# One group of edges moved, routing in four chunks, and a last dense tile by column halves

## The chip, the cores and the metric

The program runs on one core of one Trainium2 chip, as one launch. The metric is device time in microseconds (us) of a whole execution. Three runs of the kernel before took 1525.8, 1527.35 and 1531.21 us; the median is 1527.35 us.

## The reference, cut to what matters

The input is 1250 nodes of 1024 features and 40,000 edges sorted by destination. Three blocks share one normalized input: a graph convolution in two layers, a linear attention with 16 heads (8 pairs here), and behind both a mixture of 8 experts in which each node goes to two.

```
xn = layernorm(x)
# graph: agg[dst] += xw[src] * dinv[src] * dinv[dst], two layers, batch norm between them
g  = relu(gcn(relu(batchnorm(gcn(xn + pe, W1))), W2))
# attention, per head:  q' = relu(q @ proj), k' = relu(k @ proj)
m  = (q' @ (k'^T v)) / (q' @ sum(k') + 1e-8), then @ Wo + bo
x  = x + g + m
# experts: logits = layernorm(x) @ Wr^T; the two highest, softmax of the two
x  = x + sum over the two of  weight * (silu(gate) * value) @ W2[e]^T
```

## The kernel before, in words

**Numbers.** Products are in float32 as three products of a high and a low part (`COMBOS`): the low part is what is left of the value when the high one is taken off. So a tile that leaves PSUM is read twice, by ScalarE for the high part and after it by VectorE for the low one. Nodes come in 10 tiles of 125 (`NT`, `T`), features in 8 blocks of 128 (`KD`).

**Order.** `steps()` writes out one list, `ORDER`, of keys such as `("Q", 3)`. Each engine walks this list and takes the keys that it has a part in, strictly in this order. `FULL`, `ACTED` and `DVED` number them, and engines wait on semaphores for these numbers. Two large PSUM tensors (`slot`) alternate; `places_of()` gives each key its slot. A key in `INNER` takes the slot that isn't the current one and does not turn the alternation over. `free_slot` makes TensorE wait until the former content of the slot has been read.

**Edges.** The adjacency matrix is built from 80 groups of 500 edges. `EO` (VectorE) makes eight one-hot tiles for a group, `group_product` (TensorE, L1605) multiplies them in four matmuls into one of two small PSUM tensors, `E` (ScalarE) copies the result to a stage, and GpSimd adds it in DRAM (L811), one at a time. `groups_within()` shares the groups over the large products. Within a slab product (`slab_product`, L1728) the groups stand behind the blocks that `PARTS` names; those past the fourth are put elsewhere by `EP`.

**Attention pair.** For pair p: keys' features `KK` and their sums `KV`, query features `QP`, transposes `S`, then the key projection `K` of pair p+1 (5 groups: four inside, the fifth by `EP` behind it), `AT(p,0)`, query features `QP(p,1,0)` and `QP(p,1,1)`, one in each slot, and the query projection `Q` of pair p+1 (2 groups inside, behind blocks 3 and 6), with `AT(p,1)` inside. `Q(p+1)` uses the slot of `QP(p,1,0)`.

**Dense tiles.** Behind the second graph layer, `N(i)` is the dense product of node tile i: 8 blocks x 3 combinations x 2 column halves = 48 matmuls of 512 columns (L1876). VectorE then adds input and attention (`xm`, for tile i made ahead), bias (`acc<-slot,b2b`), takes relu and sum (L1449), statistics (L1452, L1454), `LN2` (square root on ScalarE, one Newton step), and `FL` writes the normalized tile `flat`. `FT(i)` transposes it on TensorE (L1671, 8 transposes), and both engines evict it into `big`. In the list `FT(i-1)` stands behind `N(i)`, and takes the other slot; so `N(i+1)` has the slot of `N(i)`.

**Routing.** `CHUNKS` splits the ten tiles into (0-3), (4-6), (7-9). Per chunk: `R` router product (L1889, 16 matmuls of up to 500 columns; for the last chunk 16 over two tiles and 16 over the last tile), ScalarE copies it to `lgt`; `RT` transposes it (L1615) and ScalarE copies it to `lg`; `RK` ranks (VectorE, seven operations up to `sel`); `PX` counts earlier nodes of each expert by small matmuls over all earlier tiles (L1630 to L1644); `RW` makes the weights, with an exponential on ScalarE; `SL` makes the list positions `spots`. GpSimd then issues one scatter per tile and choice into `list_d` (L836). When all 20 have landed, SP reads the eight lists (L770), GpSimd gathers the nodes of an expert (L856), and TensorE begins with their transposes (L1932). While this goes on, SP loads the first expert weights.

## Time and profile before

| | us |
|---|---|
| median of three runs | 1527.35 |
| profiled execution, device time | 1526.58 |
| its span, first to last instruction | 1524.9 |
| TensorE busy in the span | 1423.5 |
| VectorE busy | 846.3 |
| ScalarE busy | 531.2 |
| GpSimd busy | 183.0 |

The rows are of the profiled execution. Its device time is 1.7 us above its span and 0.8 us below the median of the runs. PE is TensorE, PEld its weight loads, DVE is VectorE, ACT ScalarE, POOL GpSimd, and SP the engine that issues most transfers. Times in a trace are counted from the first instruction.

### The profile page before, as it was taken

The numbers are of one execution on the slowest core, as the hardware profiler recorded it, in microseconds if no ns is written. First come the engines' busy times: TensorE is split into PE (matmuls) and PEld (weight loads), VectorE is DVE, ScalarE is ACT, GpSimd is POOL, SyncE is SP. The second block draws the span as 40 slices with busy tenths as digits, with TensorE's granted clock in tenths as the row PEclk, the third lists the DMA queues.
The fourth block names the chain that finished last, engine by engine and source line by source line (L and its number), as shares of the span: only waits on it lengthen the run. The fifth ranks groups of instructions, "written<-read, shape, count | busy, mean of one in ns | idle before, by whom it ended". The sixth has DMA issues, their size and how long they took to land.

```text
span 1524.9 us, 20038 instructions
## 1 busy us (share of the span) xinstructions
PE 1423.5 (93%) x7735; PEld 1307.4 (86%) x7735; DVE 846.3 (55%) x1535; ACT 531.2 (35%) x617; POOL 183.0 (12%) x182
## 2 busy tenths in 40 slices
PE   6999899999999999999999999999999839999996
PEld 5888889889998898899999999999777639888885
DVE  7464677777777777723666323354667534443330
ACT  4333344354344444423112133322111134544441
POOL 0112210110100101000000000000002252222311
PEclk9999999999999999999999999999999859999998
DMA  9765333242331434768343032221654667887863
GB/s 311 233 160 120 64 62 73 37 81 60 59 78 27 94 78 130 277 150 221 85 131 84 15 110 94 81 80 45 189 158 134 161 175 201 206 218 194 189 153 78
DMA packets 97186, 194.33 MB, mean 127 GB/s; under 512 B 31715, under 2 KB 62426, under 8 KB 95373
## 3 DMA queue, kind: packets, MB, share of 16 engines
q1 hardware_dynamic: 76324, 145.83, 32.6%
q0 software_dynamic: 20768, 47.22, 17.1%
q8 instruction: 62, 1.02, 0.3%
q14 instruction: 32, 0.26, 0.1%
HBM read 129.78 MB, written 73.13 MB: 133 GB/s over the span
## 4 chain that ended last, share of the span: by engine, by line
PE 69%; DMA 13%; DVE 8%; ACT 4%; issue 2%; SPq 1%; POOL 1%; POOLq 0%; ACTq 0%; DVEq 0%
PE slot L1728 24%; PE slot L1800 12%; DMA adj_d<-stage 7%; PE slot L1949 7%; PE slot L1876 6%; PE slot L1917 6%; PE kvb L1949 3%; PE kvb L1840 3%; PE slot L1932 2%; DMA adj_d<-eye_dram 2%; PE slot L1684 2%; PE slot L1825 1%; DMA mix_d<-mixn 1%; DVE qp_l L1407 1%; DVE kT L1139 1%
## 5 line engine op out<-in xcount | busy, mean ns | idle before, releaser
L1728 PE MATMUL slot<-big_hi,slab_h 128*128 128x418 f32 x768 | 195.9, 363 | 18.2 <-DVE qp_l L1407 12.0
L1728 PE MATMUL slot<-big_lo,slab_h 128*128 128x418 f32 x768 | 188.9, 354 | 0.0
L1728 PE MATMUL slot<-big_hi,slab_l 128*128 128x418 f32 x768 | 187.8, 352 | 0.0
L1728 PEld LDWEIGHTS slot<-big_hi,slab_h 128*128 128x128 f32 x768 | 138.8, 189 | 26.5 <-DVE qp_l L1407 16.1
L1728 PEld LDWEIGHTS slot<-big_hi,slab_l 128*128 128x128 f32 x768 | 144.8, 189 | 2.3
L1728 PEld LDWEIGHTS slot<-big_lo,slab_h 128*128 128x128 f32 x768 | 144.7, 189 | 2.0
L811 POOL DMA_DIRECT2D adj_d<-stage x80 | 67.1, 839 | 504.4 <-ACT stage L891 367.4
L1800 PE MATMUL slot<-adj,xs_h 125*128 125x418 f32 x480 | 118.2, 354 | 0.8 <-DVE ztmp L1139 0.5
L1800 PE MATMUL slot<-adj,xs_l 125*128 125x418 f32 x480 | 117.4, 353 | 0.0
L1143 DVE TENSOR_SCALAR oh_src<-lane,src_lo 125x125 bf16<-125x125 f16 x320 | 82.9, 259 | 29.2 <-PE kvb L1605 19.3
L1800 PEld LDWEIGHTS slot<-adj,xs_h 125*128 125x128 f32 x480 | 90.4, 189 | 2.2 <-DVE ztmp L1139 0.7
L1800 PEld LDWEIGHTS slot<-adj,xs_l 125*128 125x128 f32 x480 | 90.5, 189 | 1.2
L836 POOL DMA_INDIRECT list_d<-rec,spots x20 | 25.7, 1284 | 542.2 <-issue 513.1
L1143 DVE TENSOR_SCALAR oh_key<-key_iota,key_rel 125x240 bf16<-125x240 int16 x320 | 89.7, 281 | 0.0
L1139 DVE TENSOR_TENSOR ws_l<-ws_raw,ws_h 128x1024 fp32r<-128x1024 f32 x32 | 38.9, 1218 | 85.6 <-ACT ws_h L891 85.6
L1421 DVE RECIPROCAL nrm<-nrm 128x1254 f32<-128x1254 f32 x8 | 63.9, 7993 | 22.6 <-ACT nrm L891 22.6
L1139 DVE TENSOR_TENSOR slab_l<-slab_raw,slab_h 128x1024 fp32r<-128x1024 f32 x34 | 41.4, 1218 | 56.4 <-ACT slab_h L891 56.4
L871 POOL DMA_INDIRECT out_dram<-y,lists x32 | 49.1, 1533 | 180.8 <-ACT y L891 175.0
L1390 DVE SCALAR_TENSOR_TENSOR kk_l<-slot,kk_h 125x512 fp32r<-125x512 f32 x80 | 51.5, 686 | 29.0 <-ACT kk_h L1024 28.5
L1949 PE MATMUL slot<-xe_h,ws_h 128*128 128x420 f32 x176 | 64.4, 366 | 2.0 <-DVE xe_l L1139 2.0
L1949 PE MATMUL slot<-xe_l,ws_h 128*128 128x420 f32 x176 | 63.0, 358 | 0.0
L1949 PE MATMUL slot<-xe_h,ws_l 128*128 128x420 f32 x176 | 62.9, 357 | 0.0
(292 smaller groups left out, 2916.1 us busy)
## 6 DMA issues: line engine op xcount, KB each, us to landing
slab_raw<-slabs_dram SPq DMA_DIRECT2D x40, 512.0 KB, 3.8
ws_raw<-w_dram SPq DMA_DIRECT2D x36, 512.0 KB
adj_d<-stage POOLq DMA_DIRECT2D x81, 117.2 KB, 3.1
w_raw<-w_dram SPq DMA_DIRECT2D x9, 1024.0 KB
adj_d<-eye_dram POOLq DMA_DIRECT2D x1, 6250.0 KB, 24.2
raw<-adj_d SPq DMA_DIRECT2D x3, 1828.8 KB
dx<-x_dram SPq DMA_DIRECT2D x10, 448.0 KB
xn_d<-dx SPq DMA_DIRECT2D x10, 448.0 KB
```

Of the source, the lines that this page charges most:

```text
L811: pool.dma_start(adj_d[:, bass.ds(first, SPAN), :].rearrange("p d j -> p (d j)"), stage[g % 3][:, :], accum_op=ALU.add).then_inc(e_added, 16)
L871: pool.indirect_dma_start(out, bass.IndirectOffsetOnAxis(ap=lists[:, e, i, 0:1].bitcast(U32), axis=0), y[i][:, :], None, compute_op=ALU.ad ...
L1139: return dve.tensor_tensor(o, a, b, op)
L1143: dve.tensor_scalar(o, a, s1, None, op0)
L1390: dve.scalar_tensor_tensor(out=kk_p[k[2] % 3][1][:, :], in0=kk_bank(k), scalar=0.0, in1=kk_p[k[2] % 3][0][:, :].bitcast(F32), op0=ALU.max, ...
L1421: link(dve.reciprocal(nrm[:, :], nrm[:, :]))
L1728: mm = ten.matmul(ps[:, 512 * q:512 * q + CW], w[a][:, kt, :], big[b][:, kt, CW * q:CW * q + CW], start=(kt == 0 and c == 0), stop=(kt == ...
L1800: mm = ten.matmul(ps[:, 512 * q:512 * q + CW], xs_p[t % 2][a][:, j, :], adj[:, j, CW * q:CW * q + CW], start=(j == 0 and a == 0), stop=(j ...
L1840: mm = ten.matmul(kvb[:, FEAT * h:FEAT * h + FEAT], v_p[a][:, i, 64 * h:64 * h + 128], kk_p[i % 3][b][:, FEAT * h:FEAT * h + FEAT], start= ...
L1876: mm = ten.matmul(ps[:T, 512 * q:512 * q + 512], big[b][:, kt, T * i:T * i + T], rows_p[kt][a][:, 512 * q:512 * q + 512], start=(kt == 0 a ...
L1917: mm = ten.matmul(to[:RT_, 512 * q:512 * q + 512], a_p[a][:, f, RT_ * i:RT_ * i + RT_], w2_p[e % 2][b][:, f, 512 * q:512 * q + 512], start ...
L1949: mm = ten.matmul(ps, w[a][:, kt, :], xe[b][:, kt, :], start=(kt == 0 and c == 0), stop=(kt == KD - 1 and c == 2))
```

## The change

- In each of the pairs 1 to 7, the key projection takes 6 groups and the query projection 1. The sixth group is multiplied behind `QP(p,1,1)`, in front of the query projection; the one left in the query projection stands behind block 5. `EO` for the sixth comes in front of the eviction of `K`.
- `FT(i-1)` stands in front of `N(i)` in the list, and is issued by TensorE inside `N(i)`: behind block 5 (behind block 6 in tile 1, behind block 2 of the second half in tile 9). It is in `INNER`, so `N` alternates between the slots.
- Four chunks: (0-3), (4-6), (7-8), (9). `RT(1)` and `PX(1)` are inside `N(8)`. `R(2)` follows `N(9)`; `RT`, `RK`, `RW` of chunk 2 stand in front of `FT(9)`. The last chunk's router product has the tokens as the stationary operand, so its result needs no transpose. `RW` is split: `RX` is its part behind the exponential. `PX` reads a running count (`counts`) in one matmul in place of one for each earlier tile.
- The last dense product goes by column halves: 24 matmuls for the first half, then 24 for the second. `NA` on VectorE treats the first half meanwhile.

```diff
-CHUNKS = ((0, 4), (4, 7), (7, 10))
+CHUNKS = ((0, 4), (4, 7), (7, 9), (9, 10))
...
-        share[("K", p)], share[("Q", p)] = 5, 2
+        share[("K", p)], share[("Q", p)] = 6, 1
...
-PARTS = {0: (), 2: (3, 6), 4: (3, 4, 6, 7), 5: (2, 3, 5, 6)}
+PARTS = {0: (), 1: (5,), 4: (3, 4, 6, 7), 6: (2, 3, 5, 6)}
...
-        behind = WITHIN[("K", p + 1)][4]
+        first, second = WITHIN[("K", p + 1)][4:]
         o += with_split(("K", p + 1), [("VL", p + 1)], copied=2)
-        o += [("AT", p, 0), ("EP", behind), ("E", behind), ("QP", p, 1, 0), ("QP", p, 1, 1)]
+        o += [("AT", p, 0), ("EP", first), ("E", first), ("QP", p, 1, 0), ("QP", p, 1, 1),
+              ("EP", second), ("E", second)]
         o += with_split(("Q", p + 1), [("AT", p, 1)], copied=0) + [("RC", p)]
...
+    in_front = {6: [("RT", 0), ("RK", 0)], 7: [("PX", 0), ("RW", 0), ("RX", 0), ("SL", 0)],
+                8: [("RT", 1), ("RK", 1), ("RW", 1), ("RX", 1)], NT - 1: [("NA", NT - 1)]}
     for i in range(NT):
-        if i == 6:
-            o += [("RT", 0), ("RK", 0)]
-        if i == 7:
-            o += [("PX", 0), ("RW", 0), ("SL", 0)]
-        if i == 9:
-            o += [("RT", 1), ("RK", 1)]
-        o.append(("N", i))
+        o += in_front.get(i, [])
         if i:
             o.append(("FT", i - 1))
-        o += [("LN2", i), ("FL", i)]
-        if i == 5:
-            o.append(("R", 0))
         if i == 8:
-            o.append(("R", 1))
-    o += [("PX", 1), ("RW", 1), ("SL", 1), ("FT", NT - 1), ("R", LAST), ("RT", LAST), ("RK", LAST), ("PX", LAST),
-          ("RW", LAST), ("SL", LAST)]
+            o += [("PX", 1), ("SL", 1)]
+        o += [("N", i), ("LN2", i)]
+        if i == NT - 1:
+            o.append(("R", 2))
+        o.append(("FL", i))
+        if i in (5, 7):
+            o.append(("R", (i - 5) // 2))
+    o += [("RT", 2), ("RK", 2), ("RW", 2), ("FT", NT - 1), ("PX", 2), ("RX", 2), ("SL", 2),
+          ("R", LAST), ("RK", LAST), ("RW", LAST), ("PX", LAST), ("RX", LAST), ("SL", LAST)]
...
+INNER |= {("FT", i) for i in range(NT - 1)}
+AMID = {(6, 3): ("RT", 0), (7, 3): ("PX", 0), (8, 1): ("RT", 1), (8, 6): ("PX", 1)}
 PSUM_KINDS = {"DG", "DT", "Z", "H", "HT", "XT", "V", "K", "Q", "KK", "QP", "AT",
...
                 elif kind == "R":
                     a, b = CHUNKS[k[1]]
+                    if k[1] == LAST:
+                        copy(lg2[:, 2 * EXP * a:2 * EXP * b], ps[:T, 0:2 * EXP]).then_inc(act_done, 1)
+                        continue
                     if k[1]:
...
+                elif k == ("N", NT - 1):
+                    i = k[1]
+                    half = slice(512, D)
+                    dve.wait_ge(psum_full, u)
+                    tt(acc[i % 2][:, half], ps[:T, half], b2b[:, half], ALU.add).then_inc(dve_done, 1)
+                    dve.wait_ge(dve_done, DVED[k])
+                    link(dve.scalar_tensor_tensor(out=acc[i % 2][:, half], in0=acc[i % 2][:, half], scalar=0.0,
+                                                  in1=xm[i % 2][:, half], op0=ALU.max, op1=ALU.add))
+                    link(dve.bn_stats(l2st[:, i, 6:12], acc[i % 2][:, half]))
+                    link(dve.bn_aggr(l2mv[:, 2 * i:2 * i + 2], l2st[:, i, :].rearrange("p (q c) -> p q c", c=6)))
+                    ts(nw[:T, 6 * i:6 * i + 1], l2mv[:, 2 * i + 1:2 * i + 2], LN_EPS, ALU.add).then_inc(ln2_var, 1)
...
+                elif kind == "NA":
+                    i = k[1]
+                    half = slice(0, 512)
+                    dve.wait_ge(acc_stored[i % 2], LAND * (i // 2))
+                    dve.wait_ge(xm_landed[i % 2], 2 * LAND * (i // 2 + 1))
+                    link(tt(xm[i % 2][:, :], xm[i % 2][:, :], x_t[i % 2][:, :], ALU.add))
+                    dve.wait_ge(dense_half, 1)
+                    link(tt(acc[i % 2][:, half], sums[SLOT[("N", i)]][:T, half], b2b[:, half], ALU.add))
+                    link(dve.scalar_tensor_tensor(out=acc[i % 2][:, half], in0=acc[i % 2][:, half], scalar=0.0,
+                                                  in1=xm[i % 2][:, half], op0=ALU.max, op1=ALU.add))
+                    dve.bn_stats(l2st[:, i, 0:6], acc[i % 2][:, half])
+                elif kind in ("RK", "RW", "RX", "SL"):
...
+                        if c < LAST:
+                            link(dve.tensor_reduce(count_f, sel[:, 0:EXP * b].rearrange("p (j e) -> p e j", e=EXP),
+                                                   AX.X, ALU.add))
+                            dve.tensor_copy(counts[:, EXP * c + EXP:EXP * c + 2 * EXP], count_f).then_inc(counted, 1)
+                    elif kind == "RX":
...
+            def router_product(k):
+
+                a, b = CHUNKS[k[1]]
+                free_slot(k)
+                ps = sums[SLOT[k]]
+                first = T * a - (T * (b - a)) % 2
+                ten.wait_ge(dve_done, DVED[("FT", b - 1)])
+                if k[1] == LAST:
+                    for kt in range(KD):
+                        for q in range(2):
+                            mm = ten.matmul(ps[:T, 0:2 * EXP], big[q][:, kt, T * a:T * b],
+                                            wr_p[q][:, 2 * EXP * kt:2 * EXP * kt + 2 * EXP],
+                                            start=(kt == 0 and q == 0), stop=(kt == KD - 1 and q == 1))
+                    mm.then_inc(psum_full, 1)
+                    return
+                for kt in range(KD):
+                    for q in range(2):
+                        mm = ten.matmul(ps[:, 0:T * b - first], wr_p[q][:, 2 * EXP * kt:2 * EXP * kt + 128],
+                                        big[q][:, kt, first:T * b],
+                                        start=(kt == 0 and q == 0), stop=(kt == KD - 1 and q == 1))
+                mm.then_inc(psum_full, 1)
...
-                    ten.wait_ge(dve_done, DVED[("RK", c - 1)])
-                    for j in range(a):
-                        ten.matmul(to.rearrange("p (j e) -> p j e", e=EXP), before_t[:, T:],
-                                   sel[:, EXP * j:EXP * j + EXP].unsqueeze(1).to_broadcast([T, b - a, EXP]),
-                                   start=(j == 0), stop=False, skip_group_check=True)
-                        if c == LAST:
-                            ten.matmul(kvb[:T, 384:384 + EXP], before_t[:, T:], sel[:, EXP * j:EXP * j + EXP],
-                                       start=False, stop=False, skip_group_check=True)
+                    ten.wait_ge(counted, c)
+                    count = counts[:, EXP * c:EXP * c + EXP]
+                    ten.matmul(to.rearrange("p (j e) -> p j e", e=EXP), before_t[:, T:],
+                               count.unsqueeze(1).to_broadcast([T, b - a, EXP]),
+                               start=True, stop=False, skip_group_check=True)
+                    if c == LAST:
+                        ten.matmul(kvb[:T, 384:384 + EXP], before_t[:, T:], count,
+                                   start=False, stop=False, skip_group_check=True)
...
+                    if i == NT - 1:
+                        for q in range(2):
+                            for kt in range(KD):
+                                for c, (a, b) in enumerate(COMBOS):
+                                    mm = ten.matmul(ps[:T, 512 * q:512 * q + 512], big[b][:, kt, T * i:T * i + T],
+                                                    rows_p[kt][a][:, 512 * q:512 * q + 512],
+                                                    start=(kt == 0 and c == 0), stop=(kt == KD - 1 and c == 2))
+                                if q and kt == 2:
+                                    token_transposes(("FT", i - 1))
+                            mm.then_inc((dense_half, psum_full)[q], 1)
+                        continue
...
-                        if i in AMID and kt == 3:
-                            (logit_transposes if AMID[i][0] == "RT" else prefix_products)(AMID[i])
+                        if kt == KD - 1:
+                            mm.then_inc(psum_full, 1)
+                        if (i, kt) in AMID:
+                            inner = AMID[i, kt]
+                            (logit_transposes if inner[0] == "RT" else prefix_products)(inner)
+                        if i and kt == (6 if i == 1 else 5):
+                            token_transposes(("FT", i - 1))
+                    continue
...
```

## Rows read from the trace of the kernel before

**Rows 1.** The page: busy us (share) and instructions of each engine.

```profile
PE 1423.5 (93%) x7735; PEld 1307.4 (86%) x7735; DVE 846.3 (55%) x1535; ACT 531.2 (35%) x617; POOL 183.0 (12%) x182
```

**Rows 2.** Stretches: us, busy us of each engine (instructions), granted clock, DMA share, GB/s.

```profile
1202.00:1240.00 38.00, 10.35 (x75) 9.90 (x73) 16.73 (x53) 7.98 (x11) 18.29 (x16) 0.60 0.50 131
1210.00:1212.00 2.00, 2.00 (x11) 2.00 (x10) 1.26 (x7) 1.01 (x1) 0.41 (x1) 0.50 0.92 295
1214.00:1216.00 2.00, 1.50 (x14) 1.35 (x13) 0.00 (x0) 0.47 (x1) 1.43 (x2) 1.00 0.97 330
1224.00:1226.00 2.00, 0.00 (x0) 0.00 (x0) 0.31 (x1) 1.99 (x3) 1.69 (x2) 0.50 0.29 62
```

**Rows 3.** TensorE's waits: for whom, us in total, times, longest.

```profile
PE slot L1728 <- DVE qp_l L1407: 12.0, 14, 1.4
PE slot L1876 <- DVE acc L1139: 3.9, 6, 1.3
```

**Rows 4.** Timeline, PE, a query projection: start, us, what, idle before.

```profile
342.70 0.85 PE L1728 MATMUL slot<-big_hi,slab_h 128*128 128x418 f32 x3 [1.38 <-DVE qp_l L1407]
...
352.58 0.73 PE L1728 MATMUL slot<-big_hi,slab_l 128*128 128x418 f32 x3
353.14 0.57 PE L1605 MATMUL lsb<-oh_key,oh_src 125*125 125x240 bf16 x4
...
354.14 0.74 PE L1728 MATMUL slot<-big_lo,slab_h 128*128 128x418 f32 x3
```

**Rows 5.** Page: the one-hot group; its columns end in busy us, mean ns.

```profile
L1143 DVE TENSOR_SCALAR oh_key<-key_iota,key_rel 125x240 bf16<-125x240 int16 x320 | 89.7, 281 | 0.0
```

**Rows 6.** Timeline, DVE, eviction of the key projection.

```profile
335.48 2.94 DVE L1139 TENSOR_TENSOR kT<-slot,kT 64x1254 fp32r<-64x1254 f32 x2 [3.58 <-ACT kT L891]
```

**Rows 7.** Timeline, PE, dense tiles 2 and 3.

```profile
1093.98 0.73 PE L1876 MATMUL slot<-slab_h,big_hi 128*125 128x512 f32 x2 [1.25 <-DVE acc L1139]
...
1105.29 1.02 PE L1671 MATMUL slot<-ident,flat 125*128 125x125 f32 x8
1106.83 0.73 PE L1876 MATMUL slot<-slab_h,big_hi 128*125 128x512 f32 x2 [0.53 <-DVE acc L1139]
```

**Rows 8.** Timeline, DVE, dense tile 0: bias to normalized tile.

```profile
1085.15 1.23 DVE L1139 TENSOR_TENSOR acc<-slot,b2b 125x1024 f32<-125x1024 f32 x1 [1.53 <-DMA b2b<-b_rows_dram]
...
1090.72 0.81 DVE L1142 TENSOR_SCALAR flat<-acc,l2mv,rstd 125x1024 f32<-125x1024 f32 x1
```

**Rows 9.** Timeline, DVE, dense tile 9, the same two operations.

```profile
1201.63 1.22 DVE L1139 TENSOR_TENSOR acc<-slot,b2b 125x1024 f32<-125x1024 f32 x1 [2.22 <-PE slot L1876]
...
1207.85 0.81 DVE L1142 TENSOR_SCALAR flat<-acc,l2mv,rstd 125x1024 f32<-125x1024 f32 x1
```

**Rows 10.** Timeline, all engines, transposes of tile 9 and their eviction.

```profile
1208.81 1.90 PE L1671 MATMUL slot<-ident,flat 125*128 125x125 f32 x8 [6.08 <-DVE flat L1142]
...
1210.74 1.01 ACT L891 ACTIVATE big_hi<-slot 128x1000 fp32r<-128x1000 f32 x1 [1.04 <-PE slot L1671]
...
1211.79 1.20 DVE L1139 TENSOR_TENSOR big_lo<-slot,big_hi 128x1000 fp32r<-128x1000 f32 x1 [0.50 <-ACT big_hi L891]
```

**Rows 11.** Timeline, DVE, last chunk: first logits, selection, positions.

```profile
1216.83 0.18 DVE L1139 TENSOR_TENSOR lg<-lg 125x24 f32<-125x24 f32 x1 [3.85 <-ACT lgt L891]
...
1218.88 0.18 DVE L1143 TENSOR_SCALAR sel<-rank 125x24 f16<-125x24 f32 x1
...
1221.64 0.17 DVE L1517 CAST spots<-spots_f 125x6 uint32<-125x6 f32 x1
```

**Rows 12.** Timeline, POOL, scatters: chunk 0's third, last chunk's first and sixth.

```profile
1174.78 2.13 POOL L836 DMA_INDIRECT list_d<-rec,spots  x1 [0.30 <-issue]
...
1222.11 1.17 POOL L836 DMA_INDIRECT list_d<-rec,spots  x1 [1.90 <-DVE spots L1517]
...
1229.76 1.18 POOL L836 DMA_INDIRECT list_d<-rec,spots  x1 [0.30 <-issue]
```

**Rows 13.** Timeline, PE, the first gathered nodes.

```profile
1239.99 1.66 PE L1932 MATMUL slot<-ident,xg 105*128 105x105 f32 x8 [20.08 <-DMA xg<-flat_d,lists]
```

More of the change, by code:

```diff
@@ L196 @@
 DVE_KINDS = {"ZP", "Z", "P", "XT", "WV", "VL", "K", "QE", "KK", "S", "QP", "RC", "RH", "OT", "N", "DN", "DT",
-             "FL", "FT", "RK", "RW", "SL", "MP", "RP"}
+             "FL", "FT", "RK", "RX", "SL", "MP", "RP"}
 def numbered(kinds, order=ORDER):
@@ L411, in build @@
         sel = at("sel", R + 96896, [T, NT * EXP], F16)
+        counts = at("counts", R + 97056, [T, len(CHUNKS) * EXP], F16)
+        count_f = at("count_f", R + 97120, [T, EXP])[:, :]
         rec = at("rec", R + 97280, [T, NT, 2, 2])
@@ L521, in build @@
         ln2_var = sem("ln2_var")
+        dense_half = sem("dense_half")
+        counted = sem("counted")
         ln2_std = sem("ln2_std")
@@ L894, in _ @@
                 kind = k[0]
-                if kind not in ACT_KINDS and kind not in ("LNS", "WR", "E", "X", "DG", "DT", "LN2", "RW"):
+                if kind not in ACT_KINDS and kind not in ("LNS", "WR", "E", "X", "DG", "DT", "LN2", "RX"):
                     continue
@@ L1242, in _ @@
                 kind = k[0]
-                if kind not in DVE_KINDS and kind not in ("BASE", "AT", "LN", "LNS", "WR", "BASE2", "EO", "XC", "XD", "H", "LN2", "DG"):
+                if kind not in DVE_KINDS and kind not in ("BASE", "AT", "LN", "LNS", "WR", "BASE2", "EO", "XC", "XD", "H", "LN2", "DG", "NA", "RW"):
                     continue
@@ L1475, in _ @@
                     if kind == "RK":
-                        dve.wait_ge(act_done, ACTED[("RT", c)])
+                        dve.wait_ge(act_done, ACTED[("R" if c == LAST else "RT", c)])
                         dve.wait_ge(const_in, 16 * 2)
@@ L1509, in _ @@
                         dve.wait_ge(psum_full, FULL[("PX", c)])
-                        dve.wait_ge(dve_done, DVED[("RW", c)])
+                        dve.wait_ge(dve_done, DVED[("RX", c)])
                         at_ = spot[:, a:b, :]
@@ L1640, in prefix_products @@
                     for j in range(a, b):
-                        ten.matmul(kvb[:T, 384:384 + EXP], before_t[:, T:], sel[:, EXP * j:EXP * j + EXP],
-                                   start=False, stop=(j == b - 1), skip_group_check=True)
+                        mm = ten.matmul(kvb[:T, 384:384 + EXP], before_t[:, T:], sel[:, EXP * j:EXP * j + EXP],
+                                        start=False, stop=(j == b - 1), skip_group_check=True)
                 for j in range(a, b - 1):
@@ L1878, in _ @@
                                                 start=(kt == 0 and c == 0), stop=(kt == KD - 1 and c == 2))
-                        if i in AMID and kt == 3:
-                            (logit_transposes if AMID[i][0] == "RT" else prefix_products)(AMID[i])
-                elif kind == "R":
-                    a, b = CHUNKS[k[1]]
-                    first = T * a - (T * (b - a)) % 2
-                    for lo, hi in ((first, T * b),) if b < NT else ((first, T * (b - 1) - 1), (T * (b - 1) - 1, T * b)):
-                        ten.wait_ge(dve_done, DVED[("FT", (hi - 1) // T)])
-                        for kt in range(KD):
-                            for q in range(2):
-                                mm = ten.matmul(ps[:, lo - first:hi - first], wr_p[q][:, 2 * EXP * kt:2 * EXP * kt + 128],
-                                                big[q][:, kt, lo:hi],
-                                                start=(kt == 0 and q == 0), stop=(kt == KD - 1 and q == 1),
-                                                skip_group_check=True)
+                        if kt == KD - 1:
[6 more added lines that the diff above has]
+                    continue
+                elif kind == "R":
+                    router_product(k)
+                    continue
                 mm.then_inc(psum_full, 1)
```

4 lines of the change are left out of this document (1 added, 3 removed).

## The prediction

> **What bounds the kernel now.** I read the busy times of the page first: TensorE is busy 93% of the span [rows 1], so a stretch gets shorter if TensorE has less to do in it or waits less. Then the stretches: from 1202 to 1240 us it is busy for 10.35 of 38 us, at a mean granted clock of 0.60 [rows 2]; there the end is set elsewhere. Then its waits: 12.0 us for the eviction of query features in front of slab products, and 3.9 us in front of dense products for the eviction of the dense tile before [rows 3]. Last the timelines of these three places. In the tail, the last dense tile leaves PSUM at 1201.63 and is normalized at 1208.66 [rows 9], is transposed and evicted until 1212.99 [rows 10], its chunk is ranked from 1216.83 on and has its positions at 1221.81 [rows 11], six scatters are issued from 1222.11 to 1229.76 [rows 12], and TensorE starts on gathered nodes at 1239.99, after a wait of 20 us [rows 13]. The tail is one chain, of which VectorE and then GpSimd's issue of scatters are the larger parts.
>
> **Step 1, the group in front of the query projection.** TensorE stands still for 1.38 us there, until VectorE has evicted `QP(p,1,0)` [rows 4]. A group inside a slab product costs, from its first matmul to the second triple behind it, 354.14 - 353.14 = 1.00 us, where a triple alone takes 0.56: so 0.43 us [rows 4]. Put into the gap its matmuls (0.57 us with their ends) are over before the slot is free, and the query projection has one group less. 7 pairs x 0.43 = 3.0 us less. What could take it back: the eight one-hot tiles for the sixth group now come in front of the eviction of `K` on VectorE, where the high parts are the thing waited for and VectorE is idle for 3.58 us [rows 6]. Eight at no more than 0.28 us each [rows 5] are 2.2 us, so the idle time covers them; without that cover their 2.2 us would be pushed into the gap itself, and the step would cost about 2.2 - 0.4 us a pair. The stage copy moves on ScalarE from behind the block inside `Q` to behind `QP(p,1,1)`, of which nobody waits there. The queue of additions on GpSimd has the same 80 entries. Value -3.0, ends -3.0 and 0.
>
> **Step 2, transposes inside the dense product.** Now `N(i+1)` needs the slot of `N(i)`, and waits 1.25 us once and 0.53 in each of five more tiles (3.9 in total) [rows 3, 7]. With the slots alternating it needs the slot of `FT(i-1)`. From the start of eight transposes it is 1.02 us to their end [rows 7] and 2.25 from the start of ScalarE's copy to the end of VectorE's part [rows 10], so about 3.4 us with hand-overs; behind block 5 there are 12 matmuls of 11.31/48 = 0.236 us [rows 7] and the transposes themselves, 1.0 + 2.8 = 3.8 us. So the wait goes, with 0.4 us to spare. The normalized tile must be there 36 matmuls = 8.5 us into the product: VectorE needs 6.38 us from bias to `flat` [rows 8], and now begins about 0.7 us later, as the addition into `xm` (as wide as the bias of 1.22 us [rows 9]) comes behind the eviction. 7.1 us fit into 8.5. Tile 1 is the exception: its `flat(0)` ends at 1091.53 [rows 8], which is when the dense matmuls of tile 1 are nearly over, so TensorE waits for it with a block left; 1091.6 + 3.4 gives the start of tile 2 at 1095.0, where it is at 1093.98 [rows 7]: +1.0. The five waits of 0.53 go, with some 0.1 us each of re-entry: -3.2. What stood behind the last dense product in VectorE's shadow now stands ahead of its end: `FT(8)` 1.0 and `PX(1)`, a few small matmuls, 0.5: +1.5. In tiles 8 and 9 the list on VectorE is full (`RK`, `RW`, `SL` of chunk 1, then `NA`), and I expect `RT(1)` and `FT(8)` to wait together for 0.7. Sum 1.0 - 3.2 + 1.5 + 0.7 = 0.0; no row shows these two waits, so the ends are -1.0 (no wait, re-entry 0.2) and +1.5. The product of tile 9 thus still ends as VectorE's 1201.63 says. `R(1)` is as long between tiles 7 and 8 as between 8 and 9.
>
> **Step 3, the last tile by halves.** Count from A = 1201.6, when VectorE starts on the second half. Tile 0 shows 6.38 us from bias to `flat` [rows 8], tile 9 shows 7.03, as the eviction of `FT(8)` sits in between [rows 9]; it is ahead now. Three wide operations (bias, relu and sum, statistics) are halved, each by about 0.61 [rows 9]: 6.38 - 1.83 = 4.5. So `flat(9)` is ready at A + 4.5 rather than 7.0. The first half is treated beside TensorE's second half (24 matmuls, 5.7 us, against some 3 us), so it is free.
>
> **Step 4, four chunks.** TensorE transposes from A + 4.7, ScalarE copies from 1.93 later [rows 10] (at the clock of 0.50 that [rows 2] shows there) to A + 7.65. Meanwhile VectorE ranks chunk 2: seven operations took 2.23 us for three tiles [rows 11]; for two I take 1.9, and 1.4 for the weights' first part and the count: A + 7.9. Then it evicts tile 9 (1.20) until A + 9.2, finishes chunk 2 (the part behind the exponential and the positions, some 1.6 of the 2.75 us from selection to positions [rows 11]) by A + 10.9, and GpSimd issues four scatters. One takes (1229.76 - 1222.11)/5 = 1.53 with its gap in the last chunk, where one was stretched; 1.49 without that. From A + 11.2 that makes A + 17.15. The router product of tile 9 is 16 matmuls: 11 in 2.00 us at the half clock and 14 in 1.50 at the full one [rows 2] give 2.9 or 1.7; I take 2.9: A + 9.3 + 2.9 = A + 12.2. Copy 0.3, ranking of one tile 1.6 (ends 1.4 and 2.23), 2.75 to positions, 0.3 to GpSimd: A + 17.15. Both paths meet there; the better clock alone would bring nothing. The second scatter is issued at A + 18.65, or 1220.3, where the last one is issued now at 1229.76: -9.5.
>
> What follows (last scatter's landing, lists, gather) takes 10.2 us to TensorE's start [rows 12, 13] and is kept, with +0.5 for this: weight loads start when `flat(9)` is stored, 2.5 us earlier, but the scatters come 9.5 us earlier. The loads keep the transfers at 0.92 of busy or more until 1216 and 0.29 at 1224 to 1226 [rows 2]; moved by 2.5 they end at about 1221, around the last scatter. The scatter in the trace lands when they are over, so what it costs beside them is not shown: 0 to 4 us. I take 0.5, nearest to the rows, since the loads are at their end.
>
> **Sum.** -3.0 + 0.0 - 9.5 + 0.5 = -12.0. The profiled execution took 1526.58, so 1514.6; it lies 0.8 below the median, so 1515.4 on the scale of the runs. Steps 3 and 4 can't be added up separately: without the halves everything of step 4 comes 2.5 later.
>
> **Rivals.**
> - The weight loads hold the last scatters and the list reads. For it: the transfers are nearly full [rows 2]. Against: they are at their end. Price 3 us more: 1518.4. Chance 0.12.
> - Scatters are stretched by VectorE. One of chunk 0 took 2.13 beside wide VectorE work, against 1.17 [rows 12]. If each of the last six costs 0.96 more, four delay the start of the last chunk by 3.8 and one more its second: 4.8 less gain, 1520.2. Against: in the last chunk six ran beside the same small operations in 7.65 us. Chance 0.07. The Trainium skill has a rule for this (SBUF - State Buffer, section "SBUF: two separate sides"): while VectorE runs in a mode that takes both ports, GpSimd is locked out of the shared port and can't write its transfer's descriptors. By that the time would be this rival's, if ranking operations ran in such a mode; the trace bears it out for chunk 0 only.
> - The group brings nothing, as one-hot work is late for the gap. For: the order on VectorE is strict. Against: 3.58 idle [rows 6]. 1518.4. Chance 0.08.
> - Step 2 brings more: no new waits and the first tile catches up, 1.5 to 2 less. 1513.6. Chance 0.09.
> - Slower: the transposes inside the product wait for `flat(i-1)` in every tile. The place is behind block 5; there are 1.4 us to spare. If additions and eviction on VectorE make `flat` 3 us later than I have it, 8 tiles lose 1.6 each, 12.8: 1528.2. It decides from 1.4 + 1.5 = 2.9 us late. Against: VectorE is idle 2.22 us in front of tile 9's bias even with a ranking ahead of it [rows 9]. Chance 0.04.
>
> **How the numbers follow.** The forecast, 1515.4, has 0.60. The range 1511 to 1521 holds all cases but the last and half of what lies below (three runs of before spread over 5 us, so the median has an error of its own). A difference of 0.3%, 4.6 us, is about what a measurement can tell from none. Faster by more than that, below 1522.8: 0.94; within 0.02; slower 0.04.
>
> **What would show it.** The changed profile should have the wait of L1728 for `qp_l` near 12 us still, but one group (L1605) inside the gap and query projections 0.43 us shorter; no wait of dense products for `acc`; one wait of some 1.7 us at the transposes in tile 1; about 4.5 us from the last half's bias to the end of `flat(9)`; three runs of scatters well ahead and the last two issued about 19 us behind that bias; the gather's wait at TensorE from 20.1 down to some 14. It is wrong if the last two scatters start later than A + 19, if they land more than 2 us after the second's end, or if the dense stretch is more than 1.5 us longer.

## The result and the profile after

The changed kernel takes 1516.9 us (median of 7 runs, 1511.9 to 1520.9) against 1529.1 us before (7 runs, 1525.8 to 1536.1): ratio 0.991, interval 0.9895 to 0.9928. The ratio makes 13.6 us less (11.0 to 16.1); the two medians lie 12.2 apart. The forecast was 1515.4, or 12.0 less. The profiled executions differ by 12.8 us (span 1512.1, device 1513.8).

This is the first part of the page. TensorE's busy time hardly moves [rows 1]; its share grows because the span is shorter.

```profile
span 1512.1 us, 20042 instructions
PE 1420.6 (94%) x7718; PEld 1305.8 (86%) x7718; DVE 852.9 (56%) x1563; ACT 533.1 (35%) x621; POOL 185.5 (12%) x182
```

Next are TensorE's waits (total, times, longest). In front of slab products 12.0 has become 9.2. The six waits of dense products for `acc`, 3.9 us [rows 3], are gone, and in their place stands one of 0.9 for the eviction of tile 0's transposes. Transposes wait for `flat` at tiles 0, 8 and 9 (before at tile 9 alone), and new is a wait of the last chunk's router product:

```profile
PE slot L1785 <- DVE qp_l L1415: 9.2, 14, 1.0
PE slot L1728 <- DVE flat L1150: 2.9, 3, 1.3
PE lsb L1654 <- DVE big_lo L1147: 2.3, 1, 2.3
PE slot L1944 <- DVE big_lo L1147: 0.9, 1, 0.9
```

Below is TensorE's timeline at one query projection, and VectorE's at the eviction of `K` ahead of it. The group (L1640) lies in the gap, which shrinks from 1.38 to 0.96 [rows 4]. VectorE's idle time ahead of `kT` falls from 3.58 to 1.46 [rows 6]: the 2.1 us of one-hot work fit into idle time.

```profile
340.50 0.58 PE L1640 MATMUL lsb<-oh_key,oh_src 125*125 125x240 bf16 x4
342.04 0.84 PE L1785 MATMUL slot<-big_hi,slab_h 128*128 128x418 f32 x3 [0.96 <-DVE qp_l L1415]
```

```profile
334.82 2.94 DVE L1147 TENSOR_TENSOR kT<-slot,kT 64x1254 fp32r<-64x1254 f32 x2 [1.46 <-ACT kT L896]
```

TensorE's timeline in the dense stage: the transposes (L1728) now stand inside a product. TensorE waits for tile 0's `flat`, and tile 2 starts after a second wait. From tile 1's transposes on there is none, up to one of 0.36 for tile 8's.

```profile
1087.80 1.05 PE L1728 MATMUL slot<-ident,flat 125*128 125x125 f32 x8 [1.23 <-DVE flat L1150]
...
1091.17 0.74 PE L1944 MATMUL slot<-slab_h,big_hi 128*125 128x512 f32 x2 [0.94 <-DVE big_lo L1147]
...
1099.70 1.02 PE L1728 MATMUL slot<-ident,flat 125*128 125x125 f32 x8
```

VectorE's timeline in the tail follows: the second half's bias, the normalized tile, positions of the third chunk, then first logits, selection and positions of the last. A is the start of the last bias, as in the prediction; here it is 1196.44. The normalized tile is ready at A + 4.7 where it was 7.0 behind A [rows 9].

```profile
1196.44 0.69 DVE L1147 TENSOR_TENSOR acc<-slot,b2b 125x512 f32<-125x512 f32 x1 [0.28 <-PE slot L1930]
...
1200.35 0.81 DVE L1150 TENSOR_SCALAR flat<-acc,l2mv,rstd 125x1024 f32<-125x1024 f32 x1
...
1206.65 0.17 DVE L1552 CAST spots<-spots_f 125x4 uint32<-125x4 f32 x1
1209.32 0.17 DVE L1147 TENSOR_TENSOR lg<-lg 125x8 f32<-125x8 f32 x1 [2.49 <-ACT lg L896]
...
1210.68 0.55 DVE L1151 TENSOR_SCALAR sel<-rank 125x8 f16<-125x8 f32 x1
...
1213.69 0.17 DVE L1552 CAST spots<-spots_f 125x2 uint32<-125x2 f32 x1
```

TensorE there: transposes of tile 9, then first and last of 16 matmuls of the last router product, then the first gathered nodes and the first expert product. The 16 take 3.35 us.

```profile
1201.31 1.04 PE L1728 MATMUL slot<-ident,flat 125*128 125x125 f32 x8 [1.26 <-DVE flat L1150]
1205.56 0.35 PE L1654 MATMUL lsb<-wr_hilo,big_hi 128*125 128x16 f32 x1 [2.28 <-DVE big_lo L1147]
...
1208.71 0.36 PE L1654 MATMUL lsb<-wr_hi,big_lo 128*125 128x16 f32 x1
...
1226.35 1.66 PE L1997 MATMUL slot<-ident,xg 105*128 105x105 f32 x8 [14.69 <-DMA xg<-flat_d,lists]
...
1236.55 0.72 PE L2014 MATMUL slot<-xe_h,ws_h 128*128 128x420 f32 x1 [2.03 <-DVE xe_l L1147]
```

GpSimd's timeline: third chunk's four scatters, the last chunk's two, the first gather. The wait of 1.41 is the row to look at: GpSimd was free at 1213.05 and the positions came 1.1 later than a row without a pause would have had them. The last scatter is issued at A + 19.2, where it was at A + 28.1 [rows 9, 12].

```profile
1207.12 1.17 POOL L841 DMA_INDIRECT list_d<-rec,spots  x1 [11.71 <-DVE spots L1552]
...
1211.57 1.18 POOL L841 DMA_INDIRECT list_d<-rec,spots  x1 [0.30 <-issue]
1214.16 1.17 POOL L841 DMA_INDIRECT list_d<-rec,spots  x1 [1.41 <-DVE spots L1552]
1215.64 1.18 POOL L841 DMA_INDIRECT list_d<-rec,spots  x1 [0.31 <-issue]
1221.81 1.00 POOL L861 DMA_INDIRECT xg<-flat_d,lists  x1 [4.99 <-DMA lists<-list_d]
```

### The profile page after: what moved, and what is told of

Same layout as the page of the kernel before. It is cut to its first block, busy times and chain, and to the rows that moved or that the text cites. A ratio compares the mean times of both kernels' runs of the same rounds, so it can differ in the third digit from the quotient of the medians.

```text
span 1512.1 us, 20042 instructions
## 1 busy us (share of the span) xinstructions
PE 1420.6 (94%) x7718; PEld 1305.8 (86%) x7718; DVE 852.9 (56%) x1563; ACT 533.1 (35%) x621; POOL 185.5 (12%) x182
## 4 chain that ended last, share of the span: by engine, by line
PE 70%; DMA 12%; DVE 9%; ACT 5%; issue 2%; SPq 1%; POOL 0%; POOLq 0%; ACTq 0%; DVEq 0%
PE slot L1785 24%; PE slot L1857 12%; PE slot L2014 7%; DMA adj_d<-stage 6%; PE slot L1982 6%; PE slot L1944 5%; PE kvb L2014 3%; PE kvb L1897 3%; DMA xn_d<-dx 2%; PE slot L1741 2%; PE slot L1882 2%; DVE qp_l L1415 1%; PE slot L1997 1%; DMA mix_d<-mixn 1%; PE slot L1919 1%
## 5 line engine op out<-in xcount | busy, mean ns | idle before, releaser
L1029 ACT ACTIVATE kk_h<-slot 125x512 fp32r<-125x512 f32 x80 | 45.9, 596 | 52.8 <-PE slot L1882 52.3
```

Source lines behind the costliest of these rows:

```text
L1029: act.activation(kk_p[k[2] % 3][0][:, :], kk_bank(k), ACT.Relu).then_inc(act_done, 1)
```

## The experiments

Single executions of the changed kernel lie up to 9 us from each other, so a term of 1 to 3 us can't be read from medians. Much of that spread comes ahead of the dense stage: tile 1 starts anywhere from 1072.4 to 1076.8 in the ten traces of kernels with the group, which are the same up to there. Counted from the start of tile 2, kernels that share a part agree within 0.2 us up to `flat(9)`, and so do two gaps a fixed number of pairs apart. The last scatter agrees as well, but for early weights, which lies 0.4 ahead of the changed kernel; the reason is given below under step 4. This table is read from the traces in that way; There is one trace of each kernel. TP, the pitch of the pairs, is the time from one query projection's gap to the one three pairs on, divided by three; "tile 1-2" is from the start of tile 1 to that of tile 2; and the last column is the time from the last scatter's issue to TensorE's start on gathered nodes.

```
                 TP     tile 1-2  A (2nd)   flat(9)   last      gathered
                                  from tile 2 ...     scatter   nodes
before           59.67  16.57     107.65    114.68    135.78    10.23
group only       59.26  16.14     107.53    114.56    135.91    10.39
inner only       59.70  17.04     105.40    111.78    132.74    10.36
three chunks     59.28  17.30     105.30    110.02    131.17    10.13
whole last       59.27  16.83     105.36    111.73    126.19    10.78
no group         59.69  16.75     105.25    109.97    124.44    10.85
changed          59.27  17.39     105.27    109.99    124.47    10.71
early weights    59.26  17.07     105.22    109.93    124.03    10.42
busy router      59.28  17.18     105.22    109.94    123.80    10.41
busy router 2    59.28  17.23     105.28    110.00    123.40    10.59
```

**The group alone**, and **the change without it.** The edit is made in the kernel before, and undone in the changed kernel; the order of the pairs goes with it in both.

```diff
-        share[("K", p)], share[("Q", p)] = 5, 2
+        share[("K", p)], share[("Q", p)] = 6, 1
```

> The kernel before with the edit to the order of the pairs alone (a group of edges between query features and query projection, the one-hot work and stage copy that go with it). Theory (a group costs 0.43 us inside a product and nothing in the gap): the starts of the query projections lie 0.39 to 0.43 us closer together per pair, the gap's wait falls from 1.37 to about 1.0, the last query projection starts 2.4 to 2.7 us earlier, and the time is 3.0 us less than before (2.4 to 3.0). Rival (the group brings nothing and what the changed kernel gained there is transfer jitter): 0, the pitch of the query projections stays at 59.66 us.

> The changed kernel with the order of the pairs as before. Theory (the parts add up): 2.7 to 3 us over the changed kernel, so some 9 us under before; the pitch of the query projections is 59.66 us again, the dense products and the tail keep their times (tail from the bias of the last half, A: last scatter near A + 19.2). Rival (the group's gain is taken back at the next wait anyway): equal to the changed kernel.

Measured: 1524.6 us against 1529.05 of its own runs of before, ratio 0.998 (0.9966 to 0.9995), 2.9 us less; without the group 1518.7, ratio 0.994 (0.9925 to 0.9956). The pitch of the pairs falls by 0.41 in one and returns to 59.69 in the other. These are the gaps of both, first the group alone, then the change without it:

```profile
340.51 0.84 PE L1729 MATMUL slot<-big_hi,slab_h 128*128 128x418 f32 x3 [0.95 <-DVE qp_l L1408]
```

```profile
342.32 0.84 PE L1784 MATMUL slot<-big_hi,slab_h 128*128 128x418 f32 x3 [1.38 <-DVE qp_l L1414]
```

Seven pairs by 0.41 are 2.9 us. The rival of transfer jitter falls. Nothing behind takes the gain back as far as the last scatter: from tile 2 to there, no group and the changed kernel are the same within 0.03.

**Transposes inside the dense product alone** (before, with whole last tile and three chunks).

```diff
+                        if i and kt == (6 if i == 1 else 5):
+                            token_transposes(("FT", i - 1))
```

> The kernel before with one thing alone: the transposes of a tile go inside the dense product of the next one (as in the changed kernel, with the eviction of tile 8 ahead of the last product's end), while group, whole last tile and three chunks are as before. Theory (from the four traces so far, counted from the start of tile 2): the tiles' pitch falls from 12.85 to 12.18 us, the start of the last bias comes 2.3 us nearer (105.3 instead of 107.65), flat(9) follows in 6.4 instead of 7.0, the last scatter is at 132.7 to 132.9 instead of 135.8, and the start of tile 2 moves up to 0.8 later behind tile 1; in all 2.1 to 2.9 us less than before. Rival (the prediction's sizes: the product's end gains nothing, as what goes is given back at tiles 8 and 9): only the 0.65 of the eviction, last scatter at 135.1, and the time as before within 1.

Measured: 1525.9, ratio 0.998 (0.9958 to 0.9995), 3.7 us less (0.8 to 6.4). In the table the product's end is 2.25 nearer to tile 2, `flat(9)` 2.9 nearer, the last scatter 3.0, and tile 2 is 0.5 later behind tile 1. VectorE's and GpSimd's rows of this kernel (A, last scatter):

```profile
1201.07 1.22 DVE L1141 TENSOR_TENSOR acc<-slot,b2b 125x1024 f32<-125x1024 f32 x1
```

```profile
1228.41 1.18 POOL L838 DMA_INDIRECT list_d<-rec,spots  x1 [0.30 <-issue]
```

The rival, which was the prediction's own sizes, falls: this part is worth 2.6 us (3.0 less 0.5 at tile 2) and not 0.65.

**The last tile whole**, and **three chunks**, each in the changed kernel.

```diff
-CHUNKS = ((0, 4), (4, 7), (7, 9), (9, 10))
+CHUNKS = ((0, 4), (4, 7), (7, 10))
```

> The changed kernel with the last dense tile in one piece, with its bias, relu, sum and statistics behind the whole of it. Theory: flat(9) comes at A + 6.4 to 6.6 instead of A + 4.72, the two last scatters 1.8 us later behind A than 19.2 (21.0), as the path over VectorE ends last; 1.8 us over the changed kernel. Rival (the four scatters of the third chunk set the start of the last two, so the halves bring only a part): at most 0.7 us over. Second rival (the halves cost TensorE a poorer order of matmuls, 0.9 us in the last product): 0.9 less of the difference.

> The changed kernel with three chunks (0-4, 4-7, 7-10) and the tail's order of before; halves, group and inner transposes stay. Theory (the sum of the prediction: 28.13 behind A before, less 2.5 for the halves, and the eviction of tile 8 is ahead of the end): last scatter at A + 25.2 to 25.6, so 6 to 6.5 us over the changed kernel. Rival (four chunks bring less, since the path over VectorE is nearly as long, and most of the gain is from the halves and the earlier eviction): 2 to 4 us over.

Measured: whole last tile 1517.3, ratio 0.993 (0.9915 to 0.9952); three chunks 1525.2, ratio 0.997 (0.9953 to 0.9987). The first can't be told from the changed kernel by its median; in the table the whole tile costs 1.7 at `flat(9)` and 1.7 at the last scatter. Three chunks cost 6.7. The last scatters of both:

```profile
1216.08 1.18 POOL L841 DMA_INDIRECT list_d<-rec,spots  x1 [0.30 <-issue]
```

```profile
1224.33 1.19 POOL L839 DMA_INDIRECT list_d<-rec,spots  x1 [0.31 <-issue]
```

The first theory holds (last scatter at A + 20.8, for 21.0). The second holds in its mechanism and is short by a little: the last scatter is at A + 25.9, where it gave 25.2 to 25.6, and 6.7 is above its 6.5. The two parts add up: halves bring 1.6 with three chunks (132.74 to 131.17) and 1.7 with four; four chunks bring 6.5 with a whole tile and 6.7 with halves.

**Weights early.** Two of the five loads go behind the store of tile 7.

```diff
+                    if j == 7:
+                        for m in range(2):
+                            load_ws(m)
```

> The changed kernel with two of the five loads of expert weights (1 of 3 MB) issued behind the store of tile 7 rather than behind the last dense product. Theory (the loads beside the last scatters and the list reads are what makes the stretch from the last scatter to TensorE's start 10.7 instead of 10.2 us): 10.2 or less again, 0.5 us less. Rival 1 (loads have nothing to do with it): 10.7. Rival 2 (their place costs the scatters' chain much more than that: every indirect write goes through the same transfers): 1 to 3 us less, the list reads issued under 2.4 us behind the last scatter instead of 2.92. Rival 3 (the loads now collide with the reads for tile 9 and delay its addition): 0.5 to 1 later at A.

Measured: 1514.4, ratio 0.990 (0.9884 to 0.9921), the changed kernel's within the intervals. The list reads are issued 2.89 us behind the last scatter (2.92 in the changed kernel, 2.88 before), and A is where it was, so rivals 2 and 3 fall. The stretches fit this (the column ahead of the last is the transfers' busy share): in the changed kernel (first two lines) the transfers are at 0.42 from 1214 to 1216 and at 0.11 from 1216 on, when the last scatter has just been issued. With early weights (third line) they are at 0.18 in the stretch from 1214, though A lies 2.4 us later in that trace.

```profile
1214.00:1216.00 2.00, 0.00 (x0) 0.00 (x0) 0.45 (x3) 0.64 (x1) 1.54 (x2) 0.50 0.42 138
1216.00:1218.00 2.00, 0.00 (x0) 0.00 (x0) 0.26 (x1) 1.99 (x3) 0.82 (x1) 0.50 0.11 2
```

```profile
1214.00:1216.00 2.00, 0.00 (x0) 0.00 (x0) 1.48 (x11) 0.20 (x1) 1.31 (x2) 0.50 0.18 31
```

Between theory and rival 1 this doesn't decide: 10.42 lies between 10.2 and 10.7. But the kernel with all added matmuls (below) has 10.29 with its loads where the changed kernel has them, so a short stretch doesn't need moved loads. What varies is the time from the list reads' issue to the first gather, 2.40 to 3.25 in the kernels of the table.

**Added matmuls ahead of the router product** (their results are unused).

```diff
+                if k[1] == LAST:
+                    keep_busy(16)
                 ten.wait_ge(dve_done, DVED[("FT", b - 1)])
```

> The changed kernel with 16 added matmuls of 240 columns (results unused) ahead of the wait of the last chunk's router product, which in the trace took 3.35 us at the half clock behind 2.28 us of standing still. The prediction said that a better clock alone would bring nothing, since GpSimd would then be the later one. Theory now (in the changed trace GpSimd was free 1.1 us before the positions of the last chunk came): if the product runs at the full clock it is 1.2 to 1.6 us shorter, and the last two scatters come 1.1 us earlier, GpSimd's wait of 1.41 gone down to 0.3; A + 18.1 instead of A + 19.2. Rival 1 (the prediction's word): nothing. Rival 2: so few matmuls don't bring the granted clock back, the product stays at 3.3 us, and their time, where it runs over the wait, adds up to 1 us.

Measured: 1513.5, ratio 0.9885 (0.9867 to 0.9903). None of the three came as stated. The added ones (first row) ran at the half clock, so the product started 1.2 us later than the eviction would have let it (A + 10.4, where it was A + 9.1 in the changed kernel). It then took 1.9 us at the full clock, and the last scatters follow without a pause.

```profile
1206.06 3.75 PE L1647 MATMUL lsb<-wr_hilo,ones_r 128*128 128x240 f32 x16
```

```profile
1216.32 1.18 POOL L841 DMA_INDIRECT list_d<-rec,spots  x1 [0.33 <-DVE spots L1552]
1217.80 1.18 POOL L841 DMA_INDIRECT list_d<-rec,spots  x1 [0.30 <-issue]
```

So the last scatter was at A + 18.6. Little of that is due to the added matmuls: here the clock had fallen ahead of the transposes of tile 9 (1.90 us instead of 1.04), and in the trace of early weights, where it had too and nothing was added, the last scatter was at A + 18.8. The third chunk's first scatter came at A + 11.2, not 10.7, in both. The second try has added ones ahead of these as well:

> The changed kernel with added matmuls of 240 columns (results unused) in two places of the tail: 9 ahead of the wait of the last tile's transposes (where TensorE stood for 1.26 us) and 12 ahead of the wait of the last chunk's router product (2.28 us). Sixteen in the second place alone ran at the half clock for 3.75 us and past the wait, the product itself then at the full one in 1.9 us; in all the last scatter came at A + 18.58 instead of A + 19.2, and there GpSimd had become the later path (0.33 us between the fourth and the fifth scatter, as within a row). Theory: with the clock kept up from the transposes on, both the positions of the third chunk (A + 10.7) and the logits of the last (product 1.9 instead of 3.35 us, from A + 9.1) come early, and the six scatters go in one row: last one at A + 10.7 + 7.4 = A + 18.1, so 1.1 us less than the changed kernel. Rival (nine matmuls don't keep the clock; the product starts at the half clock and late): A + 18.6 to 19.2, 0 to 0.6 less.

Measured: 1516.6, ratio 0.9915 (0.9896 to 0.9933). TensorE (9 added, transposes, 12 added, first and last matmul of the product) and GpSimd's last scatter:

```profile
1202.46 1.27 PE L1647 MATMUL lsb<-wr_hilo,ones_r 128*128 128x240 f32 x9
1203.71 1.07 PE L1740 MATMUL slot<-ident,flat 125*128 125x125 f32 x8
...
1205.64 1.60 PE L1647 MATMUL lsb<-wr_hilo,ones_r 128*128 128x240 f32 x12
1207.98 0.27 PE L1662 MATMUL lsb<-wr_hilo,big_hi 128*125 128x16 f32 x1 [0.74 <-DVE big_lo L1147]
...
1209.64 0.25 PE L1662 MATMUL lsb<-wr_hi,big_lo 128*125 128x16 f32 x1
```

```profile
1217.05 1.19 POOL L841 DMA_INDIRECT list_d<-rec,spots  x1 [0.31 <-issue]
```

The theory holds in the trace: product 1.8 us, six scatters in one row, the last at A + 18.1, 1.07 less. Medians can't show so little.

**Added matmuls from the last positions to the expert product.** First all 110 ahead of the gather's wait, then 95 there and 31 in the waits behind it, then that with the second router try.

```diff
+            keep_busy(95)
             ten.wait_ge(rounds_ready, 1)
```

> The changed kernel with 110 added matmuls of 240 columns (results unused) behind the last positions' products, in the 14.69 us in which TensorE waits for the gather. Theory: the transposes of gathered nodes then start at the full clock (0.9 instead of 1.66 us a group) and the first expert product is not slowed (4.6 instead of 6.8 us); where the gathers land later than a group takes, the transposes still wait, so the gain is 0.8 + 2.2 = 3.0 us at most and 1.5 to 2.2 if the waits between groups grow by what the groups lose. Rival 1 (the chain there is the gather and the evictions on ScalarE and VectorE, not TensorE): under 0.5. Rival 2 (the added matmuls run past the gather's landing and hold it up): slower by up to 2.

> The changed kernel with added matmuls (results unused) wherever TensorE waits from the last positions to the first expert product: 95 ahead of the gather's wait, 8, 5 and 4 between the transposes of gathered nodes, 14 ahead of the first expert product. With 110 in the first place alone the first transposes ran at the full clock (0.94 us) but the later ones and the first expert product at the half one again, and the stretch from the first transposes to the end of the first expert product was 16.04 instead of 16.86 us. Theory (TensorE's clock is worth something only at the last transposes and in the expert product): last transposes 0.9 instead of 1.63, product 4.6 instead of 6.66, so 2.5 to 2.8 us less than the changed kernel, 14.1 to 14.4 for that stretch. Rival (the gathers' landings and the evictions set the order, and the added matmuls get in the way of the transposes): under 1 us less, or slower.

> Both of the other two kernels of this call in one. Theory: their gains add up, 1.1 + 2.6 = 3.7 us less than the changed kernel, so some 16 us less than before. Rival (both bring little): equal to the changed kernel within 1 us.

Measured: 1515.7, ratio 0.990 (0.9883 to 0.9919); 1514.9, 0.990 (0.9885 to 0.9917); 1515.0, 0.990 (0.9886 to 0.9921). In the first kernel the transposes slow down again behind TensorE's wait for the second ones. From the first transposes to the end of the first expert product it is 16.0 us, 0.8 less than in the changed kernel, between rival 1 (under 0.5) and the theory (1.5 to 2.2):

```profile
1229.18 0.94 PE L2004 MATMUL slot<-ident,xg 105*128 105x105 f32 x8 [0.87 <-DMA xg<-flat_d,lists]
1231.69 1.27 PE L2004 MATMUL slot<-ident,xg 105*128 105x105 f32 x8 [1.57 <-DMA xg<-flat_d,lists]
1233.62 3.37 PE L2004 MATMUL slot<-ident,xg 105*128 105x105 f32 x16 [0.66 <-DMA xg<-flat_d,lists]
```

In the second it stays up, and from the first transposes to the end of the first expert product it is 13.9 us (1228.10 to 1241.97) instead of 16.9 in the changed kernel. The theory's size is right there (it gave 14.1 to 14.4); but a later product of the expert now waits for VectorE (last row; the changed kernel has no such wait), and from the transposes behind that product to the first ones of the expert after next it is 34.4 (1241.97 to 1276.36) instead of 32.5 us (1243.21 to 1275.73): 1.9 of 3.0 are given back.

```profile
1234.32 0.91 PE L2007 MATMUL slot<-ident,xg 105*128 105x105 f32 x8 [0.60 <-DMA xg<-flat_d,lists]
...
1237.27 0.46 PE L2026 MATMUL slot<-xe_h,ws_h 128*128 128x420 f32 x1 [0.44 <-DVE xe_l L1147]
...
1259.62 0.70 PE L1989 MATMUL slot<-w_h,a_h 128*105 128x512 f32 x2 [0.76 <-DVE xe_l L1147]
```

In the third, the last scatter is again at A + 18.1, but the gathers landed further apart (waits of 1.22, 1.23 and 0.83 between the transposes), and from tile 2 to the end of the span it is 420.3 us against 420.9 in the changed kernel. That says little: the eight traces of kernels with all parts but perhaps the group have 418.5 to 421.1 there. None of the three can be told from the changed kernel by its time.

## Why the prediction was right

**Step 1**, forecast -3.0: 7 x 0.41 = -2.9, by the mechanism and cover named. One sign was put wrongly: the waits of L1728 for `qp_l` were to stay near 12 us and are 9.2, as the group's matmuls count as busy time inside the gap.

**Step 2**, forecast 0.0, ends -1.0 and +1.5: -1.6, outside its ends. Its first term (tile 2, +1.0) was +0.7 (17.10 us from tile 1 to 2 as a mean of eight traces of the table, 16.36 of two): waits of 1.23 and 0.94 in the changed kernel, where I had one of 1.7. Behind tile 2 I had -3.2 + 1.5 + 0.7 = -1.0, and it was -2.25 to -2.43 in the kernels with this part. From the transposes of tile 1 to those of tile 4 it is 35.99 instead of 38.37 us, 0.79 a tile: the wait of 0.53 and 0.26 more, which was put down to re-entry with 0.1. Five times 0.16 makes 0.8. The wait in tile 9 was 0.36 (none with a whole last tile) and none stood at `RT(1)`, against 0.7 for both. The rest, 0.2, has no row. The rival that step 2 brings 1.5 to 2 more (0.09) is what happened in size; its reason, no new waits, is not: there were three. The slower rival did not come near: transposes waited for `flat` in tile 0 (1.23) and tile 8 (0.36) alone.

**Step 3**, forecast A + 4.5: A + 4.7. A half-width operation takes 0.69 us where the forecast halved 1.22 to 0.61, three times. The eviction of tile 8 ahead of the end is worth 0.65 (inner only: 2.9 less at `flat(9)`, 2.25 at A), the halves 1.7.

**Step 4**, forecast last scatter at A + 18.65 and 9.5 less: A + 19.2 and 8.9. The positions of the last chunk came 1.1 us behind GpSimd, and not together with it. Three things make that up.

- The router product took 3.35 us for 2.9. The forecast took "11 in 2.00 us" [rows 2] for its pitch, but a stretch also counts matmuls that its edges cut, and here some of the transposes. The trace before has ten of its router matmuls in 2.13 us, which would have given 3.4:

```profile
1210.72 0.41 PE L1889 MATMUL lsb<-big_lo,wr_hi 128*128 128x250 f32 x1
...
1212.85 0.41 PE L1889 MATMUL lsb<-big_lo,wr_hi 128*128 128x250 f32 x1
```

- VectorE's `sel` of the last chunk took 0.55 us. With early weights, where the product took 3.35 as well, it took 0.17, and the last scatter was at A + 18.8:

```profile
1213.14 0.17 DVE L1154 TENSOR_SCALAR sel<-rank 125x8 f16<-125x8 f32 x1
```

- GpSimd's path was 0.5 early, since the transposes of tile 9 ran at the full clock (1.04 us) and the forecast had them at the half one. With early weights they took 1.90, and GpSimd waited for only 0.25 more than its usual pause.

So at the clock that it assumed, the forecast had the two paths right within 0.2 us, the product's 0.45 being made up elsewhere in the chain. The sentence that a better clock alone would bring nothing was wrong: with the transposes and the product both at the full clock the last scatter comes 1.07 sooner. "Steps 3 and 4 can't be added up separately" was wrong too: they add up within 0.2. And by the prediction's own sign, that the last two scatters start no later than A + 19, the last one at A + 19.2 is just beyond it.

**What follows** forecast +0.5: 10.71 for 10.23 in the two profiled runs; over three chunks it is 10.13 to 10.39 in four traces, over four chunks 10.41 to 10.85 in the six of the table, and 11.80, 11.18 and 10.29 in the three with matmuls added ahead of the gather. The last shows that the two groups overlap, so even the 0.3 isn't shown to be the change's. My reason doesn't carry it: in the changed kernel the weight loads were nearly over when the last scatter went out. The rival of weight loads (0.12), 3 us more, falls; the cause of what varies stays open.

**Stretched scatters** (0.07) did not happen to the last six, 1.17 to 1.18 each, with ranking beside them. But they did in chunk 1, as in chunk 0 [rows 12]; VectorE's row beside each:

```profile
1184.10 1.23 DVE L1147 TENSOR_TENSOR xm<-xm,x_t 125x1024 f32<-125x1024 f32 x1 [0.23 <-DVE spots L1552]
1186.62 1.22 DVE L1468 SCALAR_TENSOR_TENSOR acc<-acc,xm 125x1024 f32<-125x1024 f32 x1
```

```profile
1184.17 2.20 POOL L841 DMA_INDIRECT list_d<-rec,spots  x1 [4.25 <-DVE spots L1552]
1186.68 2.22 POOL L841 DMA_INDIRECT list_d<-rec,spots  x1 [0.30 <-issue]
```

Each of these scatters begins 0.06 or 0.07 us behind a wide operation with two inputs from SBUF and takes 1.0 us more. The Trainium skill (SBUF — State Buffer, section "SBUF: two separate sides") names such operations beside the two-port modes that I had quoted; this trace agrees with that half of its rule, and the tail has no wide operation of the kind while scatters are issued.

By the traces the sum is -2.9 (group), +0.7 (tile 2), -11.3 (tile 2 to last scatter: -3.0, -1.6 and -6.7), +0.3: -13.2, and the runs say -13.6 (-16.1 to -11.0). Behind the first gathered nodes nothing was forecast, and nothing can be read: from there to the end the thirteen traces have 284.1 to 286.7 us, in no order of the parts. The forecast of -12.0 came out near the measured time partly by luck: the gain of step 2 was put 1.6 too low and that of step 4 0.6 too high.

## What to carry to other kernels

Where runs spread by 9 us and the parts are worth 1 to 3, count in the trace from a mark just ahead of the changed stretch: kernels that share a part then mostly agree within 0.2 us, and each part's share can be read. Splitting the last chunk of a serial tail so that the issue of its first part runs beside the work for its second was worth 6.7 us, four times the halves. When two paths meet in a forecast, don't conclude from it that shortening either brings nothing: here three terms of 0.4 to 0.5 us (a product, one held operation, a clock) set them 1.1 us apart. And take a matmul's price from the distance of starts in a timeline, not from a count in a stretch.

## What was not expected of the hardware

The last router product moves 16 columns a matmul and took 0.21 us each at the granted clock of 0.50 (1.2 GHz), as long as one with 250 columns did there (the same pitch in the last product of before and of three chunks), and 0.11 at 1.00 (2.4 GHz, in the second router try), where 250 columns take 0.12. In this form narrowing the moving side bought nothing.

The clock fell either ahead of or behind the transposes of tile 9 in kernels with the same work on TensorE up to there: they took 1.04 us at the full clock in four of them, 1.90 at the half in two, and no run shows what decides it. It moves the third chunk's scatters by 0.5 us (A + 10.7 or A + 11.2).

A small VectorE operation can be held while GpSimd issues a scatter. In the four traces with 1.04, `sel` begins 0.6 us behind the start of a scatter of 1.18 and takes 0.55 or 0.56, so that both end nearly together; where it begins 0.2 to 0.4 behind one it takes 0.17. In the second router try and in the kernel with all added matmuls `hot`, which follows `sel`, is the one that begins 0.7 behind, and takes 0.47 and 0.46. But in the trace before, a `hot` that begins 0.87 behind one takes 0.17, and nothing was run on this: what holds them isn't shown.
